# FFN keys of a cross-attention and FFN layer: per pair of tiles with x as the moving side, or per tile with W_k as the moving side

## The reference

```
x = x + xattn(layernorm(x), ctx, Wq, Wk, Wv, Wout, bout)   # scores stretched by 1.5 around their mean
n = layernorm(x)
n_prev = n shifted down by one row, zeros in a batch's first row
xr = mu_r * n + (1 - mu_r) * n_prev
xk = mu_k * n + (1 - mu_k) * n_prev
r = sigmoid(xr @ W_r.T)
k_act = square(relu(xk @ W_k.T))
out = x + r * (k_act @ W_v.T)
```

## Time and profile before

| what | value |
|---|---|
| median of three runs | 743.82 us (743.12 to 744.17) |
| the profiled execution, its time | 744.54 us |
| the profiled execution, its span | 742.7 us |
| TensorE busy | 736.4 us, 99% |
| VectorE busy | 516.0 us, 69% |
| ScalarE busy | 426.8 us, 57% |
| GpSimd busy | 123.7 us, 17% |
| DMA queue of SyncE, share of 16 engines | 47.6% |

### The profile page before, as it was taken

One profiled execution on the slowest core, in us unless ns is written; L12 is line 12 of the kernel. 1 busy time (PEld: TensorE's weight loads), 2 busy tenths in 40 slices (PEclk: granted clock), 3 DMA queues, 4 the chain that ended last, 5 costly groups with the idle time before them and its releaser, 6 DMA issues.

```text
span 742.7 us, 13556 instructions
## 1 busy us (share of the span) xinstructions
PE 736.4 (99%) x3948; PEld 643.0 (87%) x3948; DVE 516.0 (69%) x1085; ACT 426.8 (57%) x1204; POOL 123.7 (17%) x279
## 2 busy tenths in 40 slices
PE   9999999999999999999999999999999999999998
PEld 8957888888988888898888889888888988888887
DVE  3678987777667766666776766677666667766662
ACT  3568865575746556564655656465665646565332
POOL 1111111202121120212112021211202121120211
PEclk9999999999999999999999999999999999999999
DMA  9966643545444353545435354543535454343301
GB/s 330 252 152 172 202 136 115 148 147 177 140 146 147 117 164 87 176 142 167 129 109 159 93 175 144 163 126 115 167 84 175 143 167 128 109 156 93 112 28 43
DMA packets 87239, 106.52 MB, mean 143 GB/s; under 512 B 9999, under 2 KB 64169, under 8 KB 87211
## 3 DMA queue, kind: packets, MB, share of 16 engines
q1 hardware_dynamic: 87172, 106.15, 47.6%
q10 hardware_dynamic: 39, 0.04, 0.0%
HBM read 58.70 MB, written 47.45 MB: 143 GB/s over the span
## 4 chain that ended last, share of the span: by engine, by line
PE 90%; SPq 5%; DVE 1%; DMA 1%; ACT 1%; issue 1%; POOL 0%; POOLq 0%; DVEq 0%
PE ffn L494 12%; PE ffn L496 12%; PE ffn L495 12%; PE scores L495 9%; PE scores L496 9%; PE scores L494 9%; PE attended L496 9%; PE attended L495 9%; PE attended L494 9%; SPq L353 3%; SPq L336 1%; PE attended L544 1%; PE attended L543 1%; DMA x_rows<-normed 1%; SPq L333 1%
## 5 line engine op out<-in xcount | busy, mean ns | idle before, releaser
L494 PE MATMUL scores<-A_hi,xT_hi 128*128 128x462 f32 x372 | 129.9, 349 | 0.8 <-DVE B_lo L973 0.8
L495 PE MATMUL scores<-A_lo,xT_hi 128*128 128x462 f32 x372 | 130.4, 351 | 0.0
L496 PE MATMUL scores<-A_hi,xT_lo 128*128 128x462 f32 x372 | 130.0, 349 | 0.0
L775 ACT ACTIVATE probs<-scores,neg_max 128x154 f32<-128x154 f32 x248 | 93.2, 387 | 46.7 <-DVE neg_max L1033 46.6
L496 PE MATMUL attended<-B_hi,pT_lo 128*128 128x512 f32 x288 | 112.5, 391 | 0.0
L495 PE MATMUL attended<-B_lo,pT_hi 128*128 128x512 f32 x288 | 112.4, 390 | 0.0
L494 PE MATMUL attended<-B_hi,pT_hi 128*128 128x512 f32 x288 | 112.1, 389 | 0.0
L1033 DVE TENSOR_REDUCE neg_max<-scores 128x3 f32<-128x462 f32 (+1 forms) x93 | 53.3, 581 | 80.9 <-PE scores L496 80.9
L1334 POOL TENSOR_SCALAR var<-stats 128x1 f32<-128x1 f32 x64 | 13.2, 206 | 462.4 <-DVE stats L979 461.3
L494 PEld LDWEIGHTS scores<-A_hi,xT_hi 128*128 128x128 f32 x372 | 70.2, 189 | 8.0 <-issue 1.7
L495 PEld LDWEIGHTS scores<-A_lo,xT_hi 128*128 128x128 f32 x372 | 70.1, 188 | 5.6
(11 more groups left out here) (171 smaller groups left out, 1583.3 us busy)
## 6 DMA issues: line engine op xcount, KB each, us to landing
prob_rows<-probs SPq DMA_DIRECT2D x32, 704.0 KB, 4.1
probs_handed<-prob_rows SPq DMA_DIRECT2D x128, 176.0 KB, 3.4
x_rows<-normed SPq DMA_DIRECT2D x61, 256.0 KB, 2.4
handed<-x_rows SPq DMA_DIRECT2D x244, 64.0 KB, 1.9
x_in<-in_x SPq DMA_DIRECT2D x32, 256.0 KB, 3.0
out<-x SPq DMA_DIRECT2D x31, 256.0 KB, 3.7
wq<-in_L_xattn_Wq SPq DMA_DIRECT2D x2, 1024.0 KB, 10.6
wout<-in_L_xattn_Wout SPq DMA_DIRECT2D x1, 2048.0 KB, 20.1
```

The lines of the kernel that those rows point to most:

```text
L494: te.matmul(psum, left[0], right[0], start=first, stop=False)
L495: te.matmul(psum, left[0], right[1], start=False, stop=False)
L496: return te.matmul(psum, left[1], right[0], start=False, stop=last)
L775: last = nc.scalar.activation(probs[:, q, cols], score_banks(t)[b][:, (h - h0) * J:(h - h0 + 1) * J], ACT.Exp, bias=neg_max[:, h:h + 1], a ...
```

## The change

The FFN works tile by tile. The keys are computed as the gate is: xk's columns are stationary and W_k moves in 512 columns, 12 matmuls a tile into one bank. Their result has rows on the partitions. So after relu and square the tile is stored to DRAM (`store_squares`), handed back by four DMAs (`hand_squares`, into a buffer of its own), and turned by VectorE (`squares_turn`); only then is it split (`squares_hi`, `squares_lo`) for the values. For the last tile TensorE turns the squares by four transposes (`turn_last_squares`). The mixed operands, `xn2T` and the squares are one tile wide and not two, and the column that a tile hands to the next one (`keep_halo`) is kept for every tile. The start, the steps and the end are written in another order on each engine. A step on TensorE is scores(t+2), attend(t), keys(t-1), gate(t-1), values(t-2). The load of W_v now waits until W_q's turns are done, since it lands where W_q lay, and the high part of W_k waits until W_v is turned.

```diff
-            def key_columns(q):
-                te.wait_ge(mixed_split["k"], 2 * q + 2)
-                for j in range(2):
...
-                    for m in (2 * j, 2 * j + 1):
-                        for c in range(DC):
-                            cols = tuple(w[:, c, m * P:(m + 1) * P] for w in WT["k"])
-                            last = three_passes(T[1 + j][:, (m % 2) * 2 * P:(m % 2 + 1) * 2 * P], cols,
-                                                (mixed_hi["k"][:, c, :], mixed_lo["k"][:, c, :]),
-                                                c == 0, c == DC - 1)
+            def key_rows(t):
+                if begun(t - 1):
+                    te.wait_ge(relu_ready, t)
...
+                te.wait_ge(mixed_split["k"], t + 1)
+                ffn_rows(T[1], (mixed_hi["k"], mixed_lo["k"]), WT["k"]).then_inc(k_done, 1)
...
+            def turn_last_squares():
+                te.wait_ge(square_ready, TILES)
+                for c in range(DC):
+                    last = te.transpose(S[1][:, c * P:(c + 1) * P], normed[:, c * P:(c + 1) * P], identity[:])
...
             def step(g, s):
-                if is_pair(q) and half == 0:
-                    gate_rows(q, 0)
-                    key_columns(q)
-                if is_pair(q) and half == 1:
-                    gate_rows(q, 1)
-                    value_rows(q, 0)
...
+                if is_last(t):
+                    value_rows(t - 3)
+                key_rows(t - 1)
+                gate_rows(t - 1, turn_last_x2 if is_last(t) else None)
+                if is_last(t - 1):
+                    turn_last_squares()
+                if not is_last(t + 1):
+                    value_rows(t - 2)
+                if is_last(t - 1):
+                    last_value_rows()
```

SyncE's step, and VectorE's two new functions:

```diff
+            def store_squares(t):
+                sp.wait_ge(square_ready, t + 1)
+                sp.dma_start(act_dram[bass.ds(t * P, P), :], act[:]).then_inc(act_stored, 16)
+            def hand_squares(t):
+                sp.wait_ge(act_stored, 16 * (t + 1))
+                if begun(t - 1):
+                    sp.wait_ge(act_turned, t)
+                hand(act_dram, t, act_landed, act_handed)
...
                 if is_tile(t + 2):
                     store_probs(t + 2)
+                if is_tile(t - 1) and not is_last(t - 1):
+                    store_squares(t - 1)
                 if is_tile(t) and not is_last(t):
                     store_x2(t)
+                if is_tile(t - 1) and not is_last(t - 1):
+                    hand_squares(t - 1)
                 if is_tile(t) and not is_last(t):
                     hand_x2(t)
...
+            def squares_turn(t):
+                dve.wait_ge(act_landed, 64 * (t + 1))
+                if begun(t - 1):
+                    dve.wait_ge(kv_done, t)
+                turn_blocks(actT[:], act_handed[:], DC).then_inc(act_turned, 1)
```

ScalarE's step (`squares` now stands ahead of `x2_norm`), VectorE's step near the end, and the start on SyncE:

```diff
+                squares(t - 1)
+                if is_tile(t) and not is_last(t):
+                    x2_norm(t, s)
                 if is_tile(t + 1):
                     for i in range(3):
                         probs_hi(t + 1, i)
...
+                x2_turn(t - 1)
+                mix_change(t - 1)
+                mix("k", t - 1)
+                if is_last(t) or is_last(t - 1):
+                    mixed_low("k", t - 1)
+                if is_last(t):
+                    add_x(t, g, s)
...
+                mix("r", t - 1)
...
+            hand_probs(4)
+            hand_squares(0)
+            hand_x2(2)
+            store_x(6)
+            store_squares(1)
+            hand_x(6)
+            hand_squares(1)
```

More of the change, by code:

```diff
@@ L600, in last_value_rows @@
                     for c in range(DC):
[L601 removed]
+                        last = three_passes(bank[:, 0:D // 2], (act_hi[:, c, :], act_lo[:, c, :]),
                                             tuple(w[:, c, cols] for w in WT["v"]), c == 0, c == DC - 1)
@@ L732, in _ @@
             attend(1)
+            scores(4)
+            attend(2)
+            key_rows(0)
+            gate_rows(0)
+            scores(5)
+            key_rows(1)
+            gate_rows(1)
+            attend(3)
+            value_rows(0)
+            key_rows(2)
+            gate_rows(2)
+            value_rows(1)
             turns(te, step)
@@ L963, in _ @@
                 probs_hi(3, i)
-            squares(0, 0)
-            turns(act_e, step, from_second=True)
+            mixed_high("k", 1)
+            open_gate(0, 0)
+            mixed_high("r", 1)
+            x_norm(6, 2)
+            for b in range(2):
+                exponentials(5, b)
+            squares_hi(0)
+            exponentials(5, 2)
+            normalise_early(5)
+            squares(1)
+            x_hi(6)
+            pack_hi(5)
+            mixed_high("k", 2)
+            open_gate(1, 1)
+            mixed_high("r", 2)
+            squares_hi(1)
+            x2_norm(3, 3)
+            for i in range(3):
+                probs_hi(4, i)
+            squares(2)
+            open_gate(2, 0)
+            turns(act_e, step)
         @block.vector
@@ L1093, in mix @@
+            def mix(w, t):
+                dve.wait_ge(delta_ready, t + 1)
+                if begun(t - 1):
+                    dve.wait_ge(r_done if w == "r" else k_done, t)
                 for c in range(DC):
-                    last = v.scalar_tensor_tensor(out=mixed[w][:, c, before], in0=change[:, c, :],
-                                                  scalar=mu[w][:, c:c + 1], in1=xn2T[:, c, before],
-                                                  op0=ALU.mult, op1=ALU.add)
+                    last = v.scalar_tensor_tensor(out=mixed[w][:, c, :], in0=delta[:, c, :], scalar=mu[w][:, c:c + 1],
+                                                  in1=xn2T[:, c, 0:P], op0=ALU.mult, op1=ALU.add)
@@ L1302, in _ @@
             for w in "kr":
[L1303 to L1306 removed]
+                mixed_low(w, 0)
             inverse_early(4)
[L1308 to L1315 removed]
+            x_turn(5)
+            normalise_late(4)
+            x_lo(5)
+            x2_turn(1)
+            pack_lo(4)
+            mix_change(1)
+            add_x(2, 0, 2)
             probs_turn(3)
+            mix("k", 1)
             for i in range(3):
                 probs_lo(3, i)
[L1319 to L1320 removed]
+            mixed_low("k", 1)
+            mix("r", 1)
+            x_statistics(6, 2, 2)
+            mixed_low("r", 1)
+            for b in range(2):
+                maxima(5, b)
+            weights_lo("v", range(0, 2))
+            squares_turn(0)
+            maxima(5, 2)
+            weights_lo("v", range(2, 4))
+            inverse_early(5)
+            squares_lo(0)
+            x2_turn(2)
+            normalise_late(5)
+            mix_change(2)
+            mix("k", 2)
+            x_turn(6)
+            x_lo(6)
+            pack_lo(5)
+            mix("r", 2)
+            mixed_low("k", 2)
+            mixed_low("r", 2)
+            squares_turn(1)
+            add_x(3, 0, 3)
+            squares_lo(1)
+            probs_turn(4)
+            open_values(0, 0)
+            for i in range(3):
+                probs_lo(4, i)
+            turns(dve, step)
             last_rows()
```

390 lines of the change are left out of this document (184 added, 206 removed).

## The result

The changed kernel takes 766.75 us (median, 765.64 to 769.08), the kernel before, run on the same chip, 744.16 us. The ratio is 1.031, with an interval from 1.029 to 1.034. I had predicted 746.0 us and a range up to 750.0: the direction was right and the size was not. The profiled execution has a span of 767.2 us where before had 742.7. It took 768.97 us, 2.2 above the median, so what is read from its trace is a little more than the usual loss.

A forecast was written before the change was run, and what follows sets the result against it. TensorE, busy 736.4 of 742.7 us, was taken as the bound, along with whether operands arrive in time. -4.95 + 0.4 + 2.85 + 4.25 - 0.33 = +2.2 us on the median of 743.82 gave 746.0 us, range 739.0 to 750.0.

The forecast's parts named there:

- 384 matmuls for 768: Key groups on TensorE: 384 matmuls of 512 columns replace 768 of 256, saving 12.9 ns each, -4.95 us.
- four transposes: TensorE's added transposes for the last tile's squares, taken at +0.4 us.
- the start: Late hand-offs make keys(2) wait 1.75 us and keys(3) 1.1 us: +2.85 us, ends 0 and 5.
- the loop: Steps between start and end: no wait counted, none expected between 160 and 690 us.
- the end: Short waits from step 30 on, for late operands and the last norm: +4.25 us, ends 1 and 6.5.
- -0.33: The one wait the kernel before had at its end, 0.33 us, which was to go.
- A step in the loop: Loop step of 21.5 us: squares land 1.5 into the next step, x2 at 3.3, keys have 3 us in hand.
- If the cover went: Caveat on the loop: without slack, each 0.1 us a step would cost 3 us in all.
- the trip blocks VectorE in every step: Loop rival: squares landing after 5 us of a step make each wait; 0.2 us in 26 steps, 751.2 us, chance 0.08.
- The rule of the Trainium skill: Key-matmul rival: 2.5 ns gap per matmul, merger worth -1.0 us instead of -4.95, time 750.0 us; chance 0.04.
- the second rival: Loop: the squares' trip blocks VectorE every step, SyncE's queue carrying a fifth more bytes; 751.2 us, chance 0.08.
- The first rival, covered ends: Start and end waits together under 3.4 us, so the gain shows; 738.9 us with none; chance 0.20.

The follow-up runs named there:

- e14: Each key matmul of 512 columns in e13 done as two of 256, nothing else changed; 747.11 us.
- e13: e12 with GpSimd's root of tile 30 ahead of keep_halo(29), and the high part of squares(29) ahead of the last norm; 742.41 us, ratio 0.9973.
- e2: The changed kernel with the squares' store ahead of the probabilities' store on SyncE; 753.87 us, ratio 1.013.
- e1: The changed kernel with add_x(t) ahead of x_turn(t+3) on VectorE; 755.09 us, ratio 1.014.
- e6: e5 with x2's hand-off ahead of the squares' in every step, VectorE's and ScalarE's squares work behind that on xk; 748.71 us, ratio 1.005.
- e9: e6 with the second norm first in ScalarE's step and in SyncE's stores; 745.57 us, ratio 1.002.
- e7: e6 with the last squares' parts in xk's free buffers, and squares(29) last on ScalarE in step 30; 749.08 us, ratio 1.006.
- e5: The changed kernel with the reorderings of e1, e2 and e3 at once; 751.47 us, ratio 1.010.
- e8: The changed kernel with 28 identity matmuls between values(0) and keys(2); 764.96 us.
- e3: The changed kernel with hand_x(6) ahead of the squares' store in SyncE's start; 758.77 us, ratio 1.019.
- e12: The kernel of e11 unchanged, run a second time; 747.12 us, ratio 1.004.
- e11: e9 with the end rewritten on all engines and e7's buffers, then VectorE and ScalarE reordered within that end; 745.61 us, ratio 1.002.

## Why the prediction was wrong, step by step

The terms of the sum, in us, against the trace of the changed kernel and the runs:

| term | predicted | measured |
|---|---|---|
| 384 matmuls for 768 | -4.95 | -4.70 (e14 against e13) |
| four transposes | +0.4 | +0.41 to the next start |
| the start | +2.85 | +7.0 |
| the loop | 0 | +13.4 |
| the end | +4.25, and -0.33 | +10.4, and -0.33 |
| sum | +2.2 | +26.2; the spans differ by 24.5 |

The start is measured from scores(5) to scores(7), 58.13 us, against 51.1 of work: two scores of 6.75, two attends of 6.58, nine FFN stages of 2.72. (e13, with one wait of 0.50 there, has 52.12.) The end is from attend(30) at 712.25 to TensorE's end at about 763.9, 51.65 us, against 41.3: two attends, nine FFN stages, 2.9 for the last values and 0.8 for the eight transposes. Some 1.7 us of it, in keys(29), is the clock. Of the 1.7 us by which the sum is too large, 0.6 is there before the change's part begins (scores(4) at 84.94 for 85.51 before). Another 0.6 is the merger: a step of before takes 21.65 us on average, 0.17 more than 21.48, which for 32 tiles is 5.3 us and not 4.7. The rest I can't place. The excess of 24.5 us is that of the profiled execution; the medians differ by 22.6.

**The step that failed is "A step in the loop".** Its sentence "A store took 704.47 - 702.44 = 2.03 us until the hand-off behind it could go" took the price from the earlier trace rows, a place near the end where no probabilities were being stored. In the loop the squares' store is always right behind 704 KB, and took 4.2. That row of before was no bound for this place; the median of `x_rows` stores on the page of before was 2.4. With 4.2 in the working the squares land at 3.7 of the next step and x2 at 5.5, which still leaves xk its time: the size alone would not have shown the loss. What was missing is the ring. I followed the squares down to the keys and found slack of 3 us; I did not follow SyncE's list on from the hand-offs to the next store of a norm, `x_turn`, `add_x` and back to the load that heads SyncE's next step. I had written "VectorE gets one turn of 0.7 us more per tile, SyncE 2.1 us of issues: both lie beside TensorE". They lie beside TensorE and inside the ring. The price and the ring belong together: in e2 the store lands in 2.1 us and the same ring costs nothing, in e1 it still takes 3.3 us and the ring is open. The sentence "If the cover went, each 0.1 us a step would be 3 us" was right in kind: 0.56 us a step made 13.4.

**The start was followed rightly and priced too low.** `x_turn(6)` came at 124.84 where I had 123.7, squares(1) ended at 120.9 for 119.9, and TensorE was done 0.5 us sooner than forecast (125.3 for 125.8). Over 1 us late on a chain of 28 us turned a wait of 1.75 before keys(2) into 3.54, as the prediction said such a delay would ("with them 1 us later it is 5 us"). Behind it came the clock, 5.25 us for keys(2) instead of 2.72, which I had in no term. keys(3) waited 0.48 and not 1.1.

**The end's waits were mostly the ones forecast.** Near the forecast: attend(31) 0.65 for 0.8, gate(30) 1.09 for 0.85, keys(31) 0.95 for 0.7. The wait of 0.8 before the last norm's turn did not come (0.1). Far off were two: keys(29) 2.34 for 0.8, where e6 and e9 showed x2's store behind the probabilities as a part of it, and then the clock. The last one, 1.46 for `act_lo`, I had at 0.25: `squares_hi(31)` waits until values(30) have read the only `act_hi`. e7 took this wait away.

**The rivals.** That the trip blocks VectorE in every step was named and had 0.08. The loop did block, but by the ring and with 0.56 us a step, not by a late landing and 0.2. The rule of the Trainium skill, page "TensorE: Matmul & The Clock Gate", section "Back-to-back issue gap", by which the merger is worth 1.0 us, is refuted for this kernel by e14, with 4.70. The bytes, for which the second rival had a fifth more, grew by 15% (106.52 to 122.78 MB), as 31 x 0.52 on 106 gives. The first rival, covered ends, needed other orders of the lists: with them (e13) the time is 742.41, where that rival had 738.9 with no wait at all.

**The way back**, by medians: e2 takes 12.9 us away (the loop), e5 2.4 more (the start), e6 2.8 (the start again), e9 3.1 (the end, and two long steps), e13 3.2 (the end): 24.3 us in all, without one transfer or instruction less.

Open stay the isolated executions of 1492.62 and 913.68 us; what the low clock costs the whole program, since e8 started its keys too late to tell; and why the loop, with the ring still closed, was 5.4 us shorter in e3 and 2.6 in e8 than in the changed kernel.

## What to carry over

When a change puts a new store and load into an in-order DMA list, don't stop where its consumer has slack: walk the list on until you meet the instruction you started from, add up once round, and compare it with a step of the bound engine. Price a store by what goes out just ahead of it on the same queue, and put the small transfer that someone waits for first. When a list is rewritten, look at every engine's list, the nearly idle one too: a root out of place on GpSimd held TensorE for 2.9 us.

## What the runs showed of the hardware

- A store of 256 KB landed in 4.2 us when issued 0.5 us behind one of 704 KB, and in 2.1 us ahead of it, with the same bytes in all.
- With waits of 3.54 and 2.34 us TensorE's granted clock fell to its level of 1.2 GHz for about 5 and 3 us of its work; behind waits of 2.72 (e5) and 2.86 us (e12) it stayed at 1.00. At the low level the spacing of 512-column matmuls was 0.427 us instead of 0.227. The Trainium skill, page "TensorE: Matmul & The Clock Gate", section "Wait — 56ns, not 53.3ns?", gives 426.7 ns for that level, and the trace agrees; for 2.4 GHz it gives 215.7, and the trace has 226.7.
- Matmuls of 256 columns were 0.12 us apart with weights (e14) or with activations (before) as the moving side; which side moves made no difference that shows.
- In one kernel (e11 and e12) one execution of each run stood far above the rest, that of 1492.62 us with TensorE at half its rate all the way.
